# A decoder layer on one core: order of TensorE's work at each change of head, and the order of the opening

## The reference

```python
# x (1, 1024, 128); context (1, 6404, 128); mask (1024, 6404)
x = layernorm(x + self_attention(x))            # 16 heads of 8, one shared K and V of 8 columns
x = layernorm(x + cross_attention(x, context))  # 16 heads of 8, own K and V, masked: score = -1e9
logits = x @ router_w.T + router_b              # 8 experts
top1, weight = argmax(softmax(logits)), max(softmax(logits))
x = layernorm(x + weight * (x @ expert_w[top1].T + expert_b[top1]))
```

## Time and profile before

| | |
|---|---|
| median of 3 runs | 510.89 us (509.74 to 511.15) |
| profiled execution | 509.33 us, span 507.6 us |
| PE busy | 482.6 us (95%) |
| DVE busy | 426.1 us (84%) |
| ACT busy | 358.9 us (71%) |
| POOL busy | 199.6 us (39%) |

### The profile page before, as it was taken

One profiled execution on the slowest core, in us unless ns is written; L12 is line 12 of the kernel. 1 busy time (PEld: TensorE's weight loads), 2 busy tenths in 40 slices (PEclk: granted clock), 3 DMA queues, 4 the chain that ended last, 5 costly groups with the idle time before them and its releaser, 6 DMA issues.

```text
span 507.6 us, 13805 instructions
## 1 busy us (share of the span) xinstructions
PE 482.6 (95%) x4140; PEld 197.3 (39%) x4140; DVE 426.1 (84%) x633; ACT 358.9 (71%) x685; POOL 199.6 (39%) x305
## 2 busy tenths in 40 slices
PE   7989999999999999888999999999999999999892
PEld 2423333333333344633444444444444444425550
DVE  5899999999999926769999899999999999902688
ACT  6238888888888877350878888888878888885220
POOL 3615898888894000132333333333333333220010
PEclk9999999999999999999999999999999999999998
DMA  3389998787500012525234111101101111011001
GB/s 96 83 264 324 305 332 295 257 299 285 224 23 13 12 54 71 178 68 147 51 62 81 41 40 39 41 26 40 38 28 40 29 41 40 26 56 48 0 0 45
DMA packets 21771, 52.56 MB, mean 104 GB/s; under 512 B 5022, under 2 KB 13376, under 8 KB 19650
## 3 DMA queue, kind: packets, MB, share of 16 engines
q1 hardware_dynamic: 18461, 22.46, 16.9%
q0 software_dynamic: 2304, 28.84, 15.1%
q10 hardware_dynamic: 932, 0.37, 0.3%
HBM read 42.10 MB, written 8.94 MB: 101 GB/s over the span
## 4 chain that ended last, share of the span: by engine, by line
PE 80%; DVE 10%; ACT 4%; issue 3%; DMA 2%; ACTq 0%; DVEq 0%; POOL 0%; POOLq 0%
PE O L1224 30%; PE ST L1452 14%; PE RT L1424 10%; PE ST L1255 9%; PE RT L1241 5%; PE RT L1564 2%; ACT prob L1047 2%; DVE mxs L746 2%; DVE mxc L896 2%; DMA Qs<-mxr 1%; PE O L1195 1%; DVE x L943 1%; DVE stat L826 1%; PE O L1220 1%; PE ST L1142 1%
## 5 line engine op out<-in xcount | busy, mean ns | idle before, releaser
L896 DVE TENSOR_REDUCE mxc<-RT 128x1024 f32 (+1 forms) x192 | 196.2, 1045 | 18.4 <-PE RT L1424 14.0
L1087 ACT ACTIVATE prob<-ST 128x512 f32<-128x512 f32 x320 | 172.0, 596 | 34.4 <-PE ST L1452 32.8
L1047 ACT ACTIVATE prob<-ST 128x512 f32<-128x512 f32 x256 | 138.6, 597 | 26.3 <-PE ST L1255 15.6
L746 DVE TENSOR_REDUCE mxs<-RT 128x2 f32<-128x1024 f32 x128 | 153.3, 1224 | 4.4 <-PE RT L1241 2.2
L1424 PE MATMUL RT<-Kr,Qs 64*128 64x128 f32 (+1 forms) x512 | 120.7, 372 | 1.9 <-DVE mxc L896 1.2
L1452 PE MATMUL ST<-Qs,Kc 64*128 64x512 f32 x320 | 120.5, 453 | 0.7 <-ACT prob L1087 0.7
L1224 PE MATMUL O<-prob,vst 128*9 128x256 f32 x1280 | 99.1, 381 | 1.6 <-ACT prob L1087 1.3
L1241 PE MATMUL RT<-Kself,Qs 64*128 64x512 f32 x256 | 89.2, 450 | 3.1 <-DVE Kself L713 1.4
L1255 PE MATMUL ST<-Qs,Kself 64*128 64x512 f32 x256 | 91.2, 450 | 0.3 <-DMA Qs<-mxr 0.3
L1224 PE MATMUL O<-prob,Vs 128*9 128x256 f32 x1024 | 79.3, 381 | 1.5 <-ACT prob L1047 0.7
L1452 PEld LDWEIGHTS ST<-Qs,Kc 64*128 64x128 f32 x320 | 53.8, 185 | 58.7 <-issue 29.9
(11 more groups left out here) (224 smaller groups left out, 344.5 us busy)
## 6 DMA issues: line engine op xcount, KB each, us to landing
big<-in_mask POOLq DMA_DIRECT2D x16, 1760.0 KB, 7.8
big<-kd SPq DMA_DIRECT2D x66, 80.0 KB
od_s<-osb SPq DMA_DIRECT2D x14, 128.0 KB, 3.4
od_x<-osb SPq DMA_DIRECT2D x14, 128.0 KB, 1.8
Qs<-qd_s SPq DMA_DIRECT2D x12, 128.0 KB, 7.2
Qs<-qd_x SPq DMA_DIRECT2D x12, 128.0 KB, 3.8
qd_s<-Vx SPq DMA_DIRECT2D x2, 512.0 KB, 3.7
qd_x<-big SPq DMA_DIRECT2D x2, 512.0 KB, 4.7
```

What stands on the lines that cost most here:

```text
L746: v.tensor_reduce(mxs[:, h % 2, c2, :].rearrange("p (f t) -> p f t", f=2)[:, :, q], RT[r % 2][:, :].rearrange("p (f k) -> p f k", f=2), AX ...
L896: v.tensor_reduce(o, src, AX.X, ALU.max).then_inc(S("x_row_free"), 1)
L1047: nc.scalar.activation(prob[:, c % SLOTS, k * HALF:(k + 1) * HALF], ST[(2 * c + k) % 3][:, :], ACT.Exp) \
L1087: nc.scalar.activation(prob[:, b, (k % 2) * HALF:(k % 2 + 1) * HALF], ST[BANK[k]][:, :], ACT.Exp) \
```

## The change

1. `next_blocks` drops the order of its own at a change of head. Column 0 of the new head, rows of unit 4, column 1, rows of unit 4, then the old head's last values, then unit 5: as inside a head. ScalarE's first exponential of the new head goes ahead of the copy of O.
2. In the opening VectorE reads the first keys before it stacks the queries; 12 unused products stand at the start and not 16; the query projections go in quarters behind rows 0 to 3, the value products behind rows 4 to 7, and unused products, one each, only behind rows 8 to 14. The value bias is added one head later.
3. SP writes head 0's max rows ahead of the first four query loads.
4. `first_bias("x")` moves behind the normalisation; three unused products go between the halves of the transposes of x.
5. The first pair's stored keys count on pen_out, and kd_out starts at 64, so nobody waits for them in the loop over pairs. ScalarE loads a register at step 126.

```diff
@@ sync @@
+            sp.sem_inc(S("kd_out"), 64)
...
+                if a == "s":
+                    max_rows(a, 0)
                 sp.wait_ge(S(a + "_q_out"), 32)
...
-            max_rows("s", 0)
...
-                k_out(0, slice(KPAD - PAIR, KPAD), k)
+                k_out(0, slice(KPAD - PAIR, KPAD), k, "pen_out")
@@ vector @@
+            dve.wait_ge(S("s_k_ready"), 1)
+            v.tensor_scalar(kz[:, 0:HALF], ST[1][:, :], rowk[:, 1:2], kcon[:, 0:1], ALU.mult, ALU.add) \
+                .then_inc(S("s_k_z"), 1)
             stack_q0("s", 0)
+            dve.wait_ge(S("s_k_z"), 1)
             dve.wait_ge(S("s_k_hi"), 1)
-            ch(v.tensor_scalar(kz[:, 0:HALF], ST[1][:, :], rowk[:, 1:2], kcon[:, 0:1], ALU.mult, ALU.add))
...
-                if r == 6:
+                if r == SELF_U:
...
             project_out("s")
+            dve.wait_ge(S("bias_ready"), 2)
+            first_bias("x")
+            settle()
+            dve.sem_inc(S("bias_moved"), 1)
@@ scalar @@
                 act.wait_ge(S("s_k_ready"), h + 1)
+                act.wait_ge(S("s_k_z"), 1)
...
+                if c == 126:
+                    p0 = act.snap(act.value_load(steer[0:1, 0:1], min_val=0, max_val=NP - MIN_PAIRS))
...
                 T0 = act.snap(n * g)
+                step_exp(T0, 0)
                 if g:
                     copy_o("x", g - 1, act.snap(T0 * NBLK + NBLK))
-                step_exp(T0, 0)
@@ tensor @@
+            def quarter_q(w, h, k, bank):
+
+                c = slice(k * 256, (k + 1) * 256)
+                mm = mmul(ST[bank][:, c], w[:, :], xT[:, h * HALF + k * 256:h * HALF + (k + 1) * 256],
+                          start=True, stop=True)
+                if k:
+                    mm.then_inc(S("s_q_ready"), 1)
...
-            warm_up(RT[0], 16)
+            warm_up(RT[0], 12)
...
-                    project_q("s", wq_s, 0, 0)
-                if r == 1:
-                    project_q("s", wq_s, 1, 1)
-                if r in (2, 3, 4, 5):
-                    project_values_s(2 * r - 4, 2 * r - 2)
-                if r >= 2:
-                    warm_up(O, 2)
+                if r < 4:
+                    quarter_q(wq_s, r // 2, r % 2, r // 2)
+                elif r < SELF_U:
+                    project_values_s(2 * r - SELF_U, 2 * r - SELF_U + 2)
+                else:
+                    warm_up(O, 1)
...
+                    if a == "s" and h == 0:
+                        warm_up(ST[2], 3)
...
-                    if g != g_before and not first:
-
-                        if h < HEADS:
-                            rows(1, 4, h, U)
-                            rows(0, 4, h, U)
-                        values(g_before, T_before, NBLK - 1, e + NCOL)
-                        have_max("x", g)
-                        for f in range(2):
-                            col(g, T, f, e + (NCOL + 1 + f - AGAIN[f]))
-                            if h < HEADS:
-                                for q in (2, 3):
-                                    rows(1 - f, 5, h, U, [q])
-                        return
+                    if first and h < HEADS:
+                        rows(1, 4, h, U)
                     if g != g_before:
-                        if h < HEADS:
-                            rows(1, 4, h, U)
                         have_max("x", g)
                     col(g, T, 0, None if first else e + (NCOL + 1 - AGAIN[0]))
-                    if g == g_before and h < HEADS:
+                    if not first and h < HEADS:
                         rows(1, 4, h, U)
                     col(g, T, 1, None if first else e + (NCOL + 2 - AGAIN[1]))
                     if h < HEADS:
                         rows(0, 4, h, U)
                     if not first:
                         values(g_before, T_before, NBLK - 1, e + NCOL)
                     if h < HEADS:
                         rows_pairwise(h, U)
```

More of the change, by code:

```diff
@@ L335, in _, with k_out @@
             load(pd.rearrange("o (a b) -> (o a) b", b=CW), penr[:, :], "pen_out")
-            def k_out(c, key, k):
+            def k_out(c, key, k, name="kd_out"):
                 for b in range(2 * k, 2 * k + 2):
                     sp.dma_start(kd[:, b * DH:(b + 1) * DH, key],
-                                 (kx_hi[c][:, :].bitcast(F32), kx_lo[c][:, :])[b // 2]).then_inc(S("kd_out"), 16)
+                                 (kx_hi[c][:, :].bitcast(F32), kx_lo[c][:, :])[b // 2]).then_inc(S(name), 16)
             sp.wait_ge(S("x_k_lo"), 1)
             for k in range(2):
-                k_out(0, slice(KPAD - PAIR, KPAD), k)
+                k_out(0, slice(KPAD - PAIR, KPAD), k, "pen_out")
             o_rows("s", HEADS - 1)
@@ L360, in _ @@
             wait_count(sp, S("kd_out"), n * 64)
-            sp.wait_ge(S("pen_out"), 16)
+            sp.wait_ge(S("pen_out"), 80)
             kdr = kd.rearrange("h r k -> (h r) k")
@@ L461, in stack @@
                 g_.tensor_tensor(o, hi.bitcast(F32), z, ALU.add).then_inc(S(name), 1)
-            pool.wait_ge(S("s_k_z"), 1)
+            pool.wait_ge(S("s_k_z"), 2)
             pool.wait_ge(S("s_k_hi"), 2)
@@ L857, in project_out @@
                     v.tensor_tensor(aT[:, w], aTr[:, w], RT[0][:, w], ALU.mult).then_inc(S(a + "_aT"), 1)
-                if a == "s":
-                    dve.wait_ge(S("bias_ready"), 2)
-                    first_bias("x")
-                    settle()
-                    dve.sem_inc(S("bias_moved"), 1)
                 for h in range(2):
@@ L966, in turned_x @@
                 if a == "s":
-                    act.wait_ge(S("pen_out"), 16)
+                    act.wait_ge(S("pen_out"), 80)
                 for h in range(2):
@@ L1052, in _ @@
             n = act.snap(n1 + 1)
-            p0 = act.snap(act.value_load(steer[0:1, 0:1], min_val=0, max_val=NP - MIN_PAIRS))
             act.wait_ge(S("vx_ones"), 1)
@@ L1289, in _ @@
             for r in range(SELF_U + LA):
-                if r == 2:
+                if r == SELF_U:
                     pe.wait_ge(S("s_q0_z"), 2)
@@ L1398, in _ @@
                 for h in range(DIRECT):
+                    if h:
+                        pe.wait_ge(S("bias_moved"), 3)
                     half_q0("x", h, f)
```

## The result

The changed kernel takes 517.98 us (median of 4 runs, 516.19 to 519.38), the kernel before in the same session 511.02: a ratio of 1.0128, 95% interval 1.009 to 1.0165. It is 1.3% slower. The forecast was 508.6. The profiled execution has a span of 515.7, against 507.6, and that is 8.1 more to account for.

A forecast was written before the change was run, and what follows sets the result against it. TensorE was taken to set the pace in the long loops. Terms -2.50 + 0.10 - 0.54 + 0.08 + 0.70 - 0.06 = -2.22 us took the median 510.89 to 508.67, say 508.6; range 505.8 to 510.9.

The forecast's parts named there:

- the query loads do not: Opening: head 2's query loads don't come earlier though wanted 2.5 us earlier; costed at nothing, bounds 0 to +2.5.
- rival C: Opening's gain taken back: query loads or a later max row stand behind a mask load; 510.7 us, chance 0.12.
- The granted clock: Opening: a clock fall would slow rows by less than VectorE's pace covers; given no size or case.
- The opening's own terms: Opening: earlier key read gains 0.75 us, back-to-back first maxima gain 1.76; in all -2.50.
- the term of 0.75: Start of opening: VectorE reads the first keys in idle time before stacking queries; gain 0.75 us, bounds 0 and 0.76.
- Change of head: Cross-attention: copy and clearing come later, mostly offset by shorter waits; +0.05 us each, 14 times, +0.70.
- rival B: Changes of cross head give nothing back, 14 x 0.19 = +2.7 us; 510.6, no change; chance 0.16.
- Column 0 needs its head's max rows 1.02 earlier than now: Change of cross head: max rows still land in time, 0.5 us to spare for the semaphore; cost nothing.
- rival D: Changes of cross head: max rows land 0.32 us too late each time, +4.5; 513.1 us, slower; chance 0.08.
- Between the attentions: VectorE's pair leaves the chain ahead of the residual sum, -0.54 us; three unused products among the transposes, +0.08.
- The register load: End of self-attention: ScalarE's load moves ahead of step 126's exponentials, on the chain; +0.1 us, bounds 0 to 0.5.
- three fifths: Whole kernel: share of the span said to lie on TensorE's products of the two attentions.

The follow-up runs named there:

- a2: Changed kernel with SP's issue of head 0's max rows put back behind the first four query loads; 513.0 us.
- b3: Kernel before with only SP's new order, head 0's max rows ahead of the first four query loads; 518.8 us, 1.2% slower.
- c1: Changed kernel with the old order at changes of cross head and the old SP order; 510.7 us, ratio 0.9981 to the kernel before.
- d1: Changed kernel with both old orders (cross head, SP) and two unused products behind each row from the fifth on; ratio 0.997 to the kernel before.
- d2: Kernel before with only the first keys read ahead and the changes around the stretch between the attentions; ratio 0.9986 to the kernel before.
- b2: Kernel before with the new cross-head order, but unit 4's first row products ahead of the max-row wait; fifteen head steps 210.3 us, total time not given.
- c2: Changed kernel with both old orders (cross head, SP) and one unused product behind each of rows four to seven; ratio 0.9972 to the kernel before.
- e1: d1 with GpSimd's second mask load held until head 1's max rows have landed; 508.3 us, ratio 0.9952 to the kernel before.

## Why the prediction was wrong

**The step that failed: "the query loads do not: they go out together with the first masks ... I cost that at nothing and keep 0 to +2.5."** It cost 7.2 (a2) to 8.1 (b3). I had found the place, and rival C named the mechanism, a query load and a later max row behind a mask load. The mistake was its price. I bounded it by how much earlier the loads are wanted (2.5), and argued that they are small. I should have asked how long such a load takes beside two masks. The chain of the kernel before has a row that says at least that size does not protect a load, and I did not use it:

```profile
46.13 7.19 DMA Qs<-mxr
```

Eight kilobytes took 7.19 us there, and the four query loads of 128 KB that were issued from 36.48 on, also beside masks, took 7.2 in the median. But these rows give a floor and not the price. At 7.2 the loads issued until 28.54 would have landed near 36, SP would have gone on ten before head 2's max rows were copied (46.26), and the loss would have been near nothing. They took 15.34 (13.71 in b3), twice as long, and no row of the trace of before says so. And the path behind was longer than one wait: query loads late, SP stands, max rows late, TensorE stands. I priced the first link only. That the order on SP makes the loss is shown (a2, b3); why these loads took twice as long as the later ones of before stays open.

**The granted clock: "I give it no case of its own."** It needed one. The fall itself costs 0.5 to 1.2 (a2 and c1 against d1), up to half of the gain of the opening. The sentence said that VectorE's pace would cover slower rows. A row pair with its unused product took 1.27 at the lower clock, against 1.13 for a maximum, in six rows: 0.8, which is what c1's loop starts later than d1's.

**The opening's own terms were right**, where nothing took them back: first maximum 12.50 (12.6); self-attention's start 2.13 earlier with the clock held (2.50). But the term of 0.75 belongs to two edits together (d2: 0.1 to 0.3 without the four products taken out in front). And 1.1 of the 2.13 went into head 0, which waits for head 1's max rows: an earlier opening moves the issue of that load forward and not the mask loads that it stands beside.

**Change of head: forecast +0.05 each, measured +0.22.** That is the size of rival B, by another mechanism in part. Terms: the copy and clearing came later, and b2 shows their net size, 1.3 / 15 = 0.09, near the +0.05. The other 0.13 came from "Column 0 needs its head's max rows 1.02 earlier than now ... That costs nothing". The prediction saw 0.5 to spare; but the load of 251.43 moved its semaphore only at 253.28, 1.85 after the issue, so 0.26 were left, and in the changed kernel the column follows the landing by 0.26 to 0.40. Head 4's landed at 301.83, with the column at 302.12. The column stands 0.31 behind the last value product of block 3 there, as at twelve of the fourteen changes and in b2 (0.32): they landed just in time for it. They did not land in time for what stood behind their wait. By the trace, TensorE's sequencer takes up the next register instruction 0.03 after the landing, and works off those of column 0 and of the row one after the other while the array has nothing. Where more of them stand behind the wait (heads 3 to 5 and 7 to 14), the row is 0.14 to 0.32 late. That is rival D's place, at less than half of its price (2.0 for 4.5). b2 shows that the row's place behind the wait makes the loss; why heads 1, 2 and 6 have fewer register instructions there I did not find out.

**Between the attentions** was right in its parts: 0.51 off the way to the sum (0.54), the pair's operation 0.29 long (under 0.4). The whole stage is 0.25 shorter (0.46 with the unused products), and the profiles without a fall of the clock there give 49.1 to 49.5 with the change and 49.6 to 49.7 without it, so the sign is right and the size near. **The register load** at step 126 was not tried alone; the last period of self-attention is 12.44 against 12.45, so it cost nothing visible, not 0.10. One reading was loose: the shares in the earlier trace rows that the prediction calls three fifths add up to 68%, over two thirds; no term hangs on it.

## What to carry to other kernels

A transfer's price is what it takes beside the others that are then in flight. The trace of before has a floor for it: look for the same kind of load at a place where the queues are full. Here that floor was 7 us and the real price 15, so a step that puts a load behind a large one needs a run and not an estimate. When a step releases a large transfer (here a max row's landing released 3.5 MB of masks), moving that step moves the large transfer ahead of everything issued since. And a product moved ahead of a wait should be the one that doesn't need it: register work behind a wait is on the path even where the data come in time.

## What the runs showed of the hardware

**Small packets beside large ones.** In the changed kernel, 28.5 to 43.9 us, the DMA view lists by queue packets, MB and share of the 16 engines (q0 holds GpSimd's masks, q1 SP's loads):

```profile
q0 software_dynamic: 325, 4.13, 86.3%
q1 hardware_dynamic: 340, 0.53, 11.6%
```

Both queues had work nearly all the time, and they moved almost the same number of packets there, 325 and 340. But the masks' packets hold 12.7 KB on average and the queries' 1.6 KB, so the queries got 11.6% of the engines' time, and half a megabyte took 15 us. The Trainium skill (DMA: Bandwidth & Descriptors, Queues, rings and completion order) says that each DMA engine takes turns between the queues that have work, a packet at a time; the equal counts agree with it. If that is the cause, a load's size says little and its number of packets counts, each of which waits for a large one. This is argued: I have not tried fewer, larger packets for the queries. Nor is it the whole. In the kernel before SP had issued 8 KB of max rows at 35.79 and four query loads from 36.48 on, and from 36.5 to 39.0 the DMA view lists the masks' queue alone:

```profile
q0 software_dynamic: 88, 1.07, 101.2%
```

So these loads waited about 3 us without a single packet, and from 36.4 to 45.6 in all SP's queue moved 904 packets and the masks' queue 171. Those counts do not look like turns. What decides between the two pictures is not known.

**The clock and unused products.** With one unused product behind each row from the fifth on, the granted clock fell to 0.50 (1.2 GHz) at 21.1 us and stayed there until 34.8; with two it stood at 1.00 (2.4 GHz) all that time (c2 and d1, same code otherwise). Taking out products that nobody uses cost 0.5 to 1.2 us of self-attention through the clock, though each row then had less to do.

**The landing of 8 KB.** In cross-attention, with no mask load in flight, a head's max rows took 1.8 to 1.9 us from issue to landing in every kernel, while only a few other loads were under way. Beside one or two mask loads, head 1's took 5.6 (e1) to 8.6 (changed kernel) and head 2's 4.5 (d2) to 10.7 (b3).
